# Attention stage of a fused two-layer kernel: values three groups behind the scores, maxima by halves of the keys, row sums in one row, weight splitting on GpSimd, the factor of q where q is rounded

## The chip, the cores and the metric

The kernel runs as one program on one core of a Trainium2 chip. The metric is device microseconds from launch to end of that core, and less is better. The core has TensorE (PE in the rows, PEld for its weight loads), VectorE (DVE), ScalarE (ACT), GpSimd (POOL) and the queue of SyncE (SP), which issues every DMA of this kernel. The engines run their own instruction lists in order and meet only at semaphores.

## The reference, cut to what matters

Two layers of a transformer over 2048 tokens of width 128: an RWKV mixer and two mixtures of experts, then attention between two gated networks with integer weights. The change touches the attention alone. What it computes (residual additions and layer norms stand around it):

```
qkv = rms_norm(x, gamma) @ w_qkv             # x: 2048 x 128, 16 heads of 64
q, k, v = split(qkv);  q = q * 64 ** -0.5
sim = einsum("bhid,bhjd->bhij", q, k)        # 2048 x 2048 for each head
attn = softmax(sim, axis=-1)
out = einsum("bhij,bhjd->bhid", attn, v)
return out @ w_out
```

Everything is float32. The kernel feeds TensorE with pairs of a rounded high part and a remainder (tiles that end in `_h` and `_l`, or `hi` and `lo`), and so gets near float32 from passes of the faster rounded type.

## The kernel before, in words

**Units of work.** A head is worked in four chunks c = 0..3 of 512 queries (CH, NC). A chunk has eight groups g = 0..7, each of 256 keys. I call "step (c, g)" what TensorE does from the scores of one group to the scores of the next. A loop runs over pairs of heads: an even head (par = 0) and an odd one (par = 1); heads 0, 1, 14 and 15 are written out around it. The file's own function `main_chunk` stands once for each engine, and the order of the code is the order of the engine's list.

**One step on TensorE.** `scores_t`: four passes of 512 columns that give transposed scores of 256 keys by 512 queries, with the negative row maxima as a 65th row of `qb`. Then `score_pair` of the *next* head: two passes that give the untransposed scores of 128 queries by 1024 keys in banks 4 and 5, only so that VectorE can take their maximum. Then `values`: four passes with the probabilities of the group PV_LAG behind. That is ten passes for a plain step. At places set by SPARE something is added: `project_v` and `project_qk` for the next heads, `turn_maxima` (a small transpose), `column_sums`, and `project_out` (one float32 product, two passes).

**The other engines in a step.** ScalarE takes the exponential twice, to `p_raw` and rounded to `p_h`. GpSimd subtracts them to `p_l` (`low_part`). VectorE adds up a quarter of a chunk's row sums (`whole_sum` in groups 0 to 3 for the chunk before, `first_half_sum` in groups 4 to 7) and takes the maximum of each score pair (`maximum`). A pair may be written only when the maximum before it is done (`s_max`), `values` waits for `p_h` and `p_l`, and `low_part` for `p_h`.

**Maxima.** Each head needs 32 pairs: 16 tiles of 128 queries by two halves of the keys, before in the order tile 0 half 0, tile 0 half 1, tile 1 half 0 and so on. PAIRS_OF_MAXIMA says how many pairs stand in each step. The rows of the change show its first chunk; in the other three there is one in every step.

**Sums.** `column_sums` turns the row sums `l_sum` (128 partitions x 512) into a [128, 4] column by four float32 products with a column of ones. `invert` takes the reciprocal on VectorE from PSUM. SP stores it (`store_inverse`), loads it back spread over 128 partitions (`load_inverse`), and GpSimd multiplies the attention output by it (`scale`). `project_out` and `add_out` follow.

**Projections.** Heads two ahead are projected in chunk 3. ScalarE copies the high part (`high_qk`), VectorE the low part (`low_qk`), and SP moves them by six DMAs for each 512 tokens to the places that the products want (`move_high`, `move_low`); the fourth part is done at the start of the next window. `high_qk_weights`/`low_qk_weights` split the weights of a head, `low_v_weights` those of a pair; q's factor of 1/8 was applied there.

**What sets the order.** Only these lists and the tables:

```
PV_LAG = 2
PAIRS_OF_MAXIMA = ((0, 0, 1, 1, 1, 2, 1, 2), (1,) * 8, (1,) * 8, (1,) * 8)
V_SPLIT = ((0, 3), (1, 0))
SCALE_GROUP = 1
COPY_GROUP = 1
```

## Time and profile before

| what | value |
|---|---|
| median of 3 runs | 2335.62 us (2335.23 to 2339.02) |
| the profiled execution, own time | 2329.67 us |
| its span, first to last instruction | 2327.9 us |
| first scores of head 0 | 674.8 us into the span |
| heads 2 to 13 | 872.6 to 2088.0 us: 1215.4 us, 12 heads |
| mean granted TensorE clock | 0.936 |

The profiled execution lies 5.95 us under the median of the timed runs, and 1.8 us of its own time lie outside the span. About 1600 us of the span are attention, in sixteen windows of about 100 us that repeat nearly to the hundredth. So a microsecond per head is worth some 15 us. In a timeline row the number in brackets is the idle time of the engine just before the instruction and what ended it. The length of a matmul row is modelled, and passes overlap: the distance of two starts tells what one costs.

### The profile page before, as it was taken

How to read it: one execution, taken by the hardware profiler on the slowest of the kernel's cores; microseconds unless marked ns; L12 is line 12 of the kernel's file. 1: busy time of each engine (PE TensorE's matmuls, PEld its weight loads, DVE VectorE, ACT ScalarE, POOL GpSimd, SP SyncE). 2: the span in 40 equal slices, each digit the busy share in tenths (PEclk: the TensorE clock that was granted, in tenths of full speed). 3: DMA queues.
4: the chain of work that ended last, by engine and by line, in shares of the span. 5: the costliest groups of instructions: out<-in, count | busy, mean ns of one | idle time of the engine just before them, and what ended most of it. 6: DMA issues, size and time to landing. Idle time of an engine off the chain costs nothing.

```text
span 2327.9 us, 30823 instructions
## 1 busy us (share of the span) xinstructions
PE 2109.7 (91%) x8706; PEld 1563.0 (67%) x8706; DVE 1862.4 (80%) x2037; ACT 1487.5 (64%) x1834; POOL 1407.1 (60%) x635
## 2 busy tenths in 40 slices
PE   6999469998779999999999999999999999999987
PEld 4777247776747676766767676676767667676654
DVE  5888867886378887888888788888888888888875
ACT  4666426664337676766777676766767667676773
POOL 1000100003038887888788788888888888888992
PEclk7999659997679999999999999999999999999997
DMA  3210003100310221303022120302212021220000
GB/s 116 62 45 18 0 0 74 45 27 15 80 31 12 64 47 38 64 14 69 12 64 48 37 64 13 69 17 60 59 26 64 18 65 26 50 64 17 10 1 18
DMA packets 68662, 94.55 MB, mean 41 GB/s; under 512 B 23200, under 2 KB 26656, under 8 KB 68256
## 3 DMA queue, kind: packets, MB, share of 16 engines
q1 hardware_dynamic: 68528, 92.80, 17.0%
q8 instruction: 80, 1.31, 0.2%
q14 instruction: 54, 0.44, 0.1%
HBM read 40.99 MB, written 1.30 MB: 18 GB/s over the span
## 4 chain that ended last, share of the span: by engine, by line
PE 66%; DVE 15%; issue 7%; ACT 4%; SPq 3%; POOL 3%; DMA 2%; DVEq 0%; ACTq 0%; POOLq 0%
PE ps L656 8%; PE ps L678 8%; PE ps L679 7%; PE ps L693 7%; PE ps L696 7%; PE ps L545 6%; PE ps L547 5%; PE ps L546 5%; DVE m_part L1365 4%; PE ps L706 4%; DVE l_sum L1359 3%; SPq L336 2%; POOL p_l L467 2%; PE ps L527 2%; ACT p_h L1041 2%
## 5 line engine op out<-in xcount | busy, mean ns | idle before, releaser
L467 POOL TENSOR_TENSOR p_l<-p_raw,p_h 128x1024 fp32r<-128x1024 f32 x512 | 1242.7, 2445 | 287.9 <-ACT p_h L1041 241.4
L1038 ACT ACTIVATE p_raw<-ps 128x1024 f32<-128x1024 f32 x512 | 564.2, 1102 | 409.1 <-PE ps L679 404.7
L1365 DVE TENSOR_REDUCE m_part<-ps 128x1 f32<-128x1024 f32 x480 | 585.7, 1220 | 215.5 <-PE ps L656 214.6
L1041 ACT ACTIVATE p_h<-ps 128x1024 fp32r<-128x1024 f32 x512 | 522.3, 1020 | 0.0
L678 PE MATMUL ps<-qa,ka 128*128 128x512 f32 x1024 | 448.6, 438 | 11.0 <-ACT p_h L1041 4.8
L693 PE MATMUL ps<-p_h,v_hl 128*128 128x512 f32 x1024 | 416.9, 407 | 29.0 <-POOL p_l L467 27.9
L679 PE MATMUL ps<-qb,kb 65*128 65x512 f32 x1024 | 412.9, 403 | 0.0
L1359 DVE TENSOR_REDUCE l_sum<-p_raw 128x128 f32<-128x1280 f32 x256 | 376.7, 1475 | 0.4
L656 PE MATMUL ps<-ka,qa 128*128 128x512 f32 x960 | 317.4, 412 | 52.2 <-DVE m_part L1365 32.9
L696 PE MATMUL ps<-p_l,v_hl 128*64 128x512 f32 x1024 | 325.5, 399 | 0.0
L1345 DVE TENSOR_REDUCE p_raw<-p_raw 128x128 f32<-128x1024 f32 x256 | 308.9, 1208 | 12.4 <-ACT p_raw L1038 12.4
L693 PEld LDWEIGHTS ps<-p_h,v_hl 128*128 128x128 f32 x1024 | 196.0, 191 | 143.4 <-issue 62.4
L656 PEld LDWEIGHTS ps<-ka,qa 128*128 128x128 f32 x960 | 177.1, 193 | 127.3 <-DVE m_part L1365 68.6
L929 ACT ACTIVATE big<-ps,b 128x512 f32<-128x512 f32 x256 | 175.3, 688 | 117.6 <-PE ps L547 117.6
L678 PEld LDWEIGHTS ps<-qa,ka 128*128 128x128 f32 x1024 | 199.0, 194 | 74.2 <-issue 33.8
L679 PEld LDWEIGHTS ps<-qb,kb 65*128 65x128 f32 x1024 | 197.9, 193 | 53.5 <-issue 15.8
L696 PEld LDWEIGHTS ps<-p_l,v_hl 128*64 128x64 f32 x1024 | 140.6, 137 | 67.6 <-issue 3.0
L1188 DVE TENSOR_TENSOR h_l<-big,h_h 128x512 fp32r<-128x512 f32 x256 | 165.6, 688 | 5.1
L443 POOL MEMSET ones<- 128x128 f32 x1 | 0.2, 204 | 247.3 <-DVE x L1202 247.3
L441 POOL TENSOR_TENSOR cen<-big 128x2048 f32<-128x2048 f32 x1 | 4.5, 4530 | 230.2 <-ACT big L947 230.2
L706 PEld LDWEIGHTS ps<-ones,l_sum 128*128 128x128 f32 x472 | 114.6, 325 | 5.4 <-issue 3.5
L1208 DVE CAST h_h<-big 128x512 fp32r<-128x512 f32 x128 | 54.6, 427 | 68.3 <-ACT big L929 68.3
(185 smaller groups left out, 2790.8 us busy)
## 6 DMA issues: line engine op xcount, KB each, us to landing
big<-g_scratch SPq DMA_DIRECT2D x64, 256.0 KB, 3.2
xnp<-r_scratch SPq DMA_DIRECT2D x59, 256.0 KB, 3.8
qa<-qk_hi SPq DMA_DIRECT2D x112, 128.0 KB, 2.4
ka<-qk_hi SPq DMA_DIRECT2D x56, 128.0 KB, 2.4
kb<-qk_hi SPq DMA_DIRECT2D x56, 128.0 KB, 2.4
ka<-xnp SPq DMA_DIRECT2D x28, 128.0 KB, 2.4
qb<-xnp SPq DMA_DIRECT2D x28, 128.0 KB, 2.4
ka<-qk_low SPq DMA_DIRECT2D x28, 128.0 KB, 2.4
```

Source lines behind the costliest of these rows:

```text
L467: nc.gpsimd.tensor_tensor(p_l[:, g % 4, :, :], slots(g), p_h[:, g % 4, :, :].bitcast(fp32), ALU.subtract).then_inc(pl_done, 1)
L656: last = mm(ps[:, 4 + b, :], qa[par][:, it * 128:it * 128 + 128], ka[par][:, chunk(2 * half + b)], start=True, stop=True)
L678: mm(st, ka[par][:, jt * 128:jt * 128 + 128], qa[par][:, ds(c * CH, CH)], start=True, stop=False)
L679: last = mm(st, kb[par][:, jt * 128:jt * 128 + 128], qb[par][:, ds(c * CH, CH)], start=False, stop=True)
L693: return mm(ps[:, bank, :], v_hl[:, par, 2 * g + j, :], p_h[:, g % 4, j, :], start=start, stop=stop)
L696: return mm(ps[0:DH, bank, :], v_hl[:, par, 2 * g + j, 0:DH], p_l[:, g % 4, j, :], start=False, stop=False)
L706: last = mm(ps[:, bank, t:t + 1], l_sum[:, :].rearrange("p (q t) -> p t q", t=TPC)[:, t, :], ones[:, 0:1], start=True, stop=True)
L1038: af(slots(g), s_t, ACT.Exp).then_inc(raw_done, 1)
L1041: af(p_h[:, g % 4, :, :], s_t, ACT.Exp).then_inc(ph_done, 1)
L1345: nc.vector.tensor_reduce(p_raw[:, ACC, cols, 0], p_raw[:, 0:ACC, cols, :].rearrange("p g n b -> p n g b"), AX.XY, ALU.add).then_inc(half_ ...
L1359: nc.vector.tensor_reduce(l_sum[:, cols], p_raw[:, ACC:GROUPS + 1, cols, :].rearrange("p g n b -> p n g b"), AX.XY, ALU.add).then_inc(all_ ...
L1365: nc.vector.tensor_reduce(m_part[:, it, half:half + 1], ps[:, 4:6, :].rearrange("p b n -> p (b n)"), AX.X, ALU.max).then_inc(s_max, 1)
```

## The change

- **PV_LAG 2 to 3.** `values` of group g - 3 follows the scores of group g. SCALE_GROUP goes from 1 to 3 and COPY_GROUP from 1 to 2.
- **Maxima by halves.** The first eight query tiles take all first halves of the keys, then all second ones (PAIR_AT). Head h+1's first pair is now in step (0, 1) and wants key chunks 0 and 1 alone; chunks 2 and 3 are wanted at pair 8, in step (1, 0). Step (0, 5) has one pair in place of two.
- **Projections later.** Part 0 of q and k goes to step (3, 3), part 1 to (3, 5), part 2 to (3, 7), part 3 to (0, 1); their low parts to (3, 4), (3, 6), (0, 0) and (0, 2).
- **Row sums.** One float32 product with a column of 1/128 gives a row [1, 512]; ScalarE copies it (`row_sums`), SP stores it and loads it back as [128, 4]; VectorE inverts that from SBUF in step (c, 0) of the chunk after. The factor 128 is taken out in `add_out`.
- **Weights.** `low_qk_weights` and `low_v_weights` go from VectorE to GpSimd, at its step (1, 1). One `qk_raw` in place of two. The factor of q is applied where q is rounded, from a column `qk_scale`, in `high_qk` and `low_qk`.

```diff
-PV_LAG = 2
+PV_LAG = 3
-PAIRS_OF_MAXIMA = ((0, 0, 1, 1, 1, 2, 1, 2), (1,) * 8, (1,) * 8, (1,) * 8)
+PAIRS_OF_MAXIMA = ((0, 1, 1, 1, 1, 1, 1, 2), (1,) * 8, (1,) * 8, (1,) * 8)
+PAIR_AT = ([(it, 0) for it in range(8)] + [(it, 1) for it in range(8)]
+           + [(it, half) for it in range(8, NT) for half in range(2)])
-LATE_LOW = 1
-INVERT_GROUP = (6, 6, 6, 4)
+LATE_LOW = {0: 2, 2: 3}
+LATE_QK = 1
...
 @block.sync
+            def store_sums(head, c):
+                sp.wait_ge(l_done, chunk_of(head, c) + 1)
+                sp.dma_start(l_scratch[ds(head, 1), chunk(c)], l_row[:, :]).then_inc(l_stored, 16)
+            def load_sums(head, c):
+                sp.wait_ge(l_stored, 16 * (chunk_of(head, c) + 1))
+                sp.dma_start(l_col[:, c % 2, :], l_scratch[ds(head, 1), chunk(c)].rearrange("a (p t) -> (a p) t", p=128)).then_inc(l_loaded, 16)
...
 @block.gpsimd
+            def low_qk_weights(par, head):
+                pool.wait_ge(qkw_hi, head + 1)
+                nc.gpsimd.tensor_tensor(qk_l[par][:, :, :], qk_raw[:, :, :], qk_h[par][:, :, :].bitcast(fp32),
+                                        ALU.subtract).then_inc(qkw_lo, 1)
...
 @block.tensor
-                for t in range(TPC):
-                    last = mm(ps[:, bank, t:t + 1], l_sum[:, :].rearrange("p (q t) -> p t q", t=TPC)[:, t, :], ones[:, 0:1],
-                              start=True, stop=True)
-                last.then_inc(l_ps, 1)
+                mm(ps[0:1, bank, :], inv_c[:, 0:1], l_sum[:, :], start=True, stop=True).then_inc(l_ps, 1)
...
 @block.scalar
+            def row_sums(head, c, bank):
+                k = chunk_of(head, c)
+                act.wait_ge(l_ps, k + 1)
...
+                af(l_row[:, :], ps[0:1, bank, :], ACT.Copy).then_inc(l_done, 1)
...
 @block.vector
-                tt(lo.bitcast(fp32r), ps[:, bank, :], hi, ALU.subtract).then_inc(lo_done, 1)
+                stt(lo.bitcast(fp32r), ps[:, bank, :], qk_scale[:, 0:1], hi, ALU.mult, ALU.subtract).then_inc(lo_done, 1)
-                dve.wait_ge(l_ps, k + 1)
+                dve.wait_ge(l_loaded, 16 * (k + 1))
-                nc.vector.reciprocal(r_col[:, c % 2, :], ps[:, bank, 0:TPC]).then_inc(r_ready, 1)
+                nc.vector.reciprocal(r_col[:, c % 2, :], l_col[:, c % 2, :]).then_inc(r_ready, 1)
-                tt(x[:, chunk(c)], x[:, chunk(c)], ps[:, bank, :], ALU.add).then_inc(out_add, 1)
+                stt(x[:, chunk(c)], ps[:, bank, :], 1.0 / C, x[:, chunk(c)], ALU.mult, ALU.add).then_inc(out_add, 1)
```

**TensorE, step (0, 5) of an even head in the loop.** Before, from the first score pair to the sums (L656 is the pair, L693 and L696 the values, L706 the sums):

```order
L656 MATMUL ps<-ka,qa 128x512 [waits s_max]
L656 MATMUL ps<-ka,qa 128x512
L693 MATMUL ps<-p_h,v_hl 128x512 [waits pl_done,ph_done]
L696 MATMUL ps<-p_l,v_hl 64x512 x2
L693 MATMUL ps<-p_h,v_hl 128x512
L654 REGISTER_ALU
L656 MATMUL ps<-ka,qa 128x512 [waits s_max]
L656 MATMUL ps<-ka,qa 128x512
L704 ISA [waits mt_done]
L706 MATMUL ps<-ones,l_sum 128x1 [waits all_sum]
L706 MATMUL ps<-ones,l_sum 128x1 x3
```

The same step of the changed kernel (L695 is the pair, L732 and L735 the values, L744 the sums):

```order
L695 MATMUL ps<-ka,qa 128x512 [waits s_max]
L695 MATMUL ps<-ka,qa 128x512
L732 MATMUL ps<-p_h,v_hl 128x512 [waits pl_done,ph_done]
L735 MATMUL ps<-p_l,v_hl 64x512 x2
L732 MATMUL ps<-p_h,v_hl 128x512
L743 ISA [waits mt_done]
L744 MATMUL ps<-l_sum,inv_c 1x512 [waits all_sum]
```

The second pair with its own wait for `s_max` is gone from the step, and four products of one column have become one of 512 columns.

**VectorE, from the last maximum of chunk 0 into chunk 1 of an even head.** Before (L1318 to L1324 split the weights, L1359 is the row sum, L1383 the residual addition):

```order
L1365 TENSOR_REDUCE m_part<-ps 128x1 [waits s_ps]
L1317 ISA
L1318 SCALAR_TENSOR_TENSOR qk_l<-qk_raw,qk_h 128x64 [waits qkw_hi]
L1320 TENSOR_TENSOR qk_l<-qk_raw,qk_h 128x64
L1323 REGISTER_ALU
L1324 TENSOR_TENSOR wv_hl<-wv_raw,wv_hl 128x128 [waits vw_hi]
L1353 ISA
L1354 REGISTER_ALU [waits raw_done]
L1359 TENSOR_REDUCE l_sum<-p_raw 128x128 [waits l_ps,half_sum]
L1383 TENSOR_TENSOR x<-x,ps 128x512 [waits out_ps]
```

The changed kernel at that place (L1401 is the maximum, L1395 the row sum, L1419 the addition, L1415 the reciprocal):

```order
L1401 TENSOR_REDUCE m_part<-ps 128x1 [waits s_ps]
L1389 ISA
L1390 REGISTER_ALU [waits raw_done]
L1395 TENSOR_REDUCE l_sum<-p_raw 128x128 [waits l_ps,half_sum]
L1419 SCALAR_TENSOR_TENSOR x<-ps,x 128x512 [waits out_ps]
L1412 REGISTER_ALU
L1415 RECIPROCAL r_col<-l_col 128x4 [waits o_scaled,l_loaded]
L1400 REGISTER_ALU
L1401 TENSOR_REDUCE m_part<-ps 128x1 [waits s_ps]
```

The weight splits have left VectorE's list here, and the reciprocal has come in ahead of the first maximum, with a wait for a DMA (`l_loaded`).

**SP, chunks 0 and 1 of an even head.** Before, from the row of maxima to the load of the inverse:

```order
L318 ISA
L320 DMA qb<-m_t 1x12x128 [waits mt_done]
L323 ISA
L324 ISA [waits r_ready]
L324 DMA r_scratch<-r_col 128x4
L327 REGISTER_ALU
L328 DMA xnp<-r_scratch 128x512 [waits r_stored]
```

The changed kernel from the same DMA on:

```order
L328 DMA qb<-m_t 1x12x128 [waits mt_done]
L331 REGISTER_ALU
L332 ISA [waits l_done]
L332 DMA l_scratch<-l_row 1x512
L335 REGISTER_ALU
L336 DMA l_col<-l_scratch 128x4 [waits l_stored]
L340 DMA r_scratch<-r_col 128x4 [waits r_ready]
L344 DMA xnp<-r_scratch 128x512 [waits r_stored]
```

Each chunk's sums now take two more DMAs, one behind the other, ahead of the two of the inverse.

## Rows read from the trace of the kernel before

**Rows 1.** The page: span, and busy time of each engine.

```profile
span 2327.9 us, 30823 instructions
PE 2109.7 (91%) x8706; PEld 1563.0 (67%) x8706; DVE 1862.4 (80%) x2037; ACT 1487.5 (64%) x1834; POOL 1407.1 (60%) x635
```

**Rows 2.** Windows: length, busy PE, PEld, DVE, ACT, POOL; clock, DMA share, GB/s.

```profile
872.60:2088.00 1215.40, 1148.86 (x4801) 846.85 (x4800) 1022.19 (x967) 849.42 (x955) 1017.54 (x445) 0.98 0.20 44
2182.40:2268.30 85.90, 75.04 (x281) 46.47 (x279) 66.83 (x49) 66.17 (x70) 83.31 (x35) 1.00 0.00 1
1281.22:1382.94 101.72, 97.90 (x425) 73.35 (x425) 83.25 (x79) 71.30 (x82) 83.43 (x37) 0.98 0.20 41
1382.94:1482.16 99.22, 92.04 (x378) 66.40 (x376) 86.32 (x82) 70.29 (x78) 85.69 (x39) 1.00 0.22 48
```

**Rows 3.** The chain of work in head 6: start, length, what.

```profile
1326.72 1.64 PE ps L706 x8
...
1334.45 0.86 PE ps L715 x2
...
1336.24 0.47 PE ps L656 x2
```

**Rows 4.** Timeline of PE, head 7: steps (0, 3) and (0, 5).

```profile
1390.84 0.39 PE L679 MATMUL ps<-qb,kb 65*128 65x512 f32 x1
1392.42 0.73 PE L656 MATMUL ps<-ka,qa 128*128 128x512 f32 x2 [1.20 <-DMA qb<-qk_low]
...
1398.83 0.39 PE L693 MATMUL ps<-p_h,v_hl 128*128 128x512 f32 x1
1399.62 0.73 PE L656 MATMUL ps<-ka,qa 128*128 128x512 f32 x2 [0.40 <-DVE m_part L1365]
```

**Rows 5.** Timeline of DVE and PE, head 7: into step (1, 1).

```profile
1409.05 1.02 DVE L1318 SCALAR_TENSOR_TENSOR qk_l<-qk_raw,qk_h 128x64 fp32r<-128x64 f32 x1
...
1411.60 0.40 PE L679 MATMUL ps<-qb,kb 65*128 65x512 f32 x1
1413.46 0.73 PE L656 MATMUL ps<-ka,qa 128*128 128x512 f32 x2 [1.46 <-DVE m_part L1365]
```

**Rows 6.** Timeline of PE, head 7: steps (1, 4) and (2, 4).

```profile
1421.36 0.63 PE L656 MATMUL ps<-ka,qa 128*128 128x512 f32 x2
1423.07 0.47 PE L693 MATMUL ps<-p_h,v_hl 128*128 128x512 f32 x1 [1.08 <-POOL p_l L467]
...
1446.31 0.47 PE L693 MATMUL ps<-p_h,v_hl 128*128 128x512 f32 x1 [0.98 <-POOL p_l L467]
```

**Rows 7.** Windows, head 6, columns as in rows 2: a stretch of low clock.

```profile
1301.60:1304.80 3.20, 3.20 (x9) 2.26 (x8) 2.35 (x2) 1.86 (x2) 2.53 (x2) 0.50 0.23 11
```

**Rows 8.** Groups by line, heads 2 to 13: count, busy us, mean ns, idle before.

```profile
L467 POOL TENSOR_TENSOR p_l<-p_raw,p_h 128x1024 fp32r<-128x1024 f32 x385 | 933.7, 2441 | 198.9 <-ACT p_h L1041 160.6 <-issue 37.2
L1365 DVE TENSOR_REDUCE m_part<-ps 128x1 f32<-128x1024 f32 x385 | 469.8, 1220 | 167.7 <-PE ps L656 166.9
...
L1359 DVE TENSOR_REDUCE l_sum<-p_raw 128x128 f32<-128x1280 f32 x192 | 283.1, 1475 | 0.0
...
L1027 ACT ACTIVATE xnp<-ps 128x512 f32<-128x512 f32 x48 | 29.3, 610 | 14.1 <-PE ps L693 14.1
...
L1335 DVE TENSOR_TENSOR qk_low<-ps,qk_hi 128x512 fp32r<-128x512 f32 x24 | 16.5, 689 | 16.7 <-ACT qk_hi L997 16.7
...
L1318 DVE SCALAR_TENSOR_TENSOR qk_l<-qk_raw,qk_h 128x64 fp32r<-128x64 f32 x12 | 12.0, 998 | 0.0
```

**Rows 9.** Before the attention, GpSimd idle: timeline, and one line's ns min/median/max.

```profile
613.55 0.22 DVE L1318 SCALAR_TENSOR_TENSOR qk_l<-qk_raw,qk_h 128x64 fp32r<-128x64 f32 x1
...
L1314 DVE SCALAR_TENSOR_TENSOR xnp<-xnp,gamma,ps x4: 749/750/750, 601.9 to 610.5; 128x512 f32<-128x512 f32 x4
```

**Rows 10.** DMA issues: count, size, median us from issue to landing.

```profile
r_scratch<-r_col SPq DMA_DIRECT2D x59, 2.0 KB, 1.7
...
mix<-in_mix SPq DMA_DIRECT2D x1, 2.5 KB, 2.9
```

More of the change, by code:

```diff
@@ L135, in macaron_kernel @@
         p_l = sb("p_l", [128, 4, 2, CH], fp32r, two)
-        qk_raw = [sb(f"qk_raw{i}", [C, 2, DH], where=two) for i in range(2)]
+        qk_raw = sb("qk_raw", [C, 2, DH], where=two)
+        qk_scale = sb("qk_scale", [128, 1], where=two)
         qk_h = [sb(f"qk_h{i}", [C, 2, DH], fp32r, two) for i in range(2)]
@@ L362, in window @@
                 for c in range(NC):
-                    summed = before(head, c, 1)
+                    scaled, summed = before(head, c, 2), before(head, c, 1)
+                    if c == 0 and late_project:
+                        move_high(head + 1, 1 - par, 2, qk_hi)
+                        move_low(head + 1, 1 - par, 2, qk_low[0])
+                    if exists(scaled[0]) and not (last and c > 0):
+                        store_inverse(*scaled)
+                        load_inverse(*scaled)
                     if c == 0 and late_project:
@@ L494, in window @@
                             low_v(head + 1, 1 - par)
+                        if (c, g) == (1, 1) and project:
+                            low_qk_weights(par, head + 2)
+                            if par == 0:
+                                low_v_weights(pair + 1)
             def attention():
+                low_qk_weights(0, 0)
+                low_v_weights(0)
+                low_qk_weights(1, 1)
                 low_v(0, 0)
@@ L862, in attention @@
                 window(PAIRS - 1, 1, False, False, False)
-                for g in (GROUPS - 2, GROUPS - 1):
+                for g in range(GROUPS - PV_LAG, GROUPS):
                     values(HEADS - 1, 1, NC - 1, g)
@@ L1058, in main_chunk @@
                             turn_maxima(head + 1 - n, n, spare_bank(c))
+                        elif kind == "sums":
+                            row_sums(*summed, spare_bank(c))
                         elif kind == "v":
@@ L1078, in attention @@
                 high_parts(3)
-                for head in range(2):
-                    high_qk_weights(head, 1)
+                high_qk_weights(0, 0)
                 high_v_weights(0)
+                high_qk_weights(1, 1)
                 for head in range(2):
@@ L1418, in main_chunk @@
                     if g == 0:
[L1419 removed]
+                        scaled, added = before(head, c, 2), before(head, c, 3)
                         if c > 0 and exists(added[0]) and not last:
@@ L1452, in attention @@
                 low_parts(3)
-                for head in range(2):
-                    low_qk_weights(head, head)
-                low_v_weights(0)
                 for head in range(2):
```

132 lines of the change are left out of this document (65 added, 67 removed).

## Prediction

> **What bounds the kernel now.** I read the page first: TensorE is busy 91% of the span, VectorE 80%, GpSimd 60% [rows 1]. That averages stages in which GpSimd has no work, so the windows come next. In heads 2 to 13 TensorE is busy 1149 of 1215 us, VectorE 1022, GpSimd 1018, ScalarE 849 [rows 2]. Per head that is 101.3 us with 95.7, 85.2, 84.8 and 70.8 busy. Nobody is saturated, and the two behind TensorE stand 16 us lower. So I ask how much of a head is TensorE's own work and how much is waiting that the busy column hides.
>
> The unit of price is the distance of two starts. In the chain a score pair of two 512-column passes advances 0.47 us, 0.235 a pass; the sums' eight pieces take 1.64, and the two passes of a float32 product of 512 columns 0.86 [rows 3]. A plain step of ten passes is 2.35, thirty-two of them 75 us. Five things above that touch the change.
>
> - Step (0, 3): a pair is due at 1390.84 + 0.235 and starts at 1392.42, 1.35 late, behind the DMA that brings the last keys [rows 4].
> - Step (0, 5): the second pair, due at 1399.06, starts at 1399.62, 0.56 late, behind the first one's maximum [rows 4].
> - The sums: 1.64 a chunk [rows 3].
> - Step (1, 1): the pair is due at 1411.83 and starts at 1413.46, 1.63 late. VectorE had the weight split, 1.02 us, ahead of its row sum [rows 5].
> - Steps (1, 4) and (2, 4) of an odd head: values are due 0.47 after the pair, at 1421.83, and start at 1423.07, 1.24 late, behind GpSimd. The second place has 0.98 of idle where the first has 1.08, so 1.14 [rows 6]. I looked for both in even heads and found none.
>
> The low clock is a sixth. One window of head 6 has the clock at 0.50, 1.2 GHz, right after the long sums of step (0, 5) and their waits [rows 7]; before it the engine had gaps in which it waited. Over the twelve heads the mean is 0.98 [rows 2]: 2% of 1215 us, 24 us of full-speed work lost, with 0.005 of rounding 18 to 30.
>
> **The change part by part**, for a pair of heads, now 202.6 us (1215.4 / 6).
>
> Keys by halves: the wait in (0, 3) goes, 2 x 1.35 = 2.7. The second half is wanted in step (1, 0), seven steps after the projection of part 3, over 16 us; six issues and a landing fit many times. A first pair a step earlier wants part 1, projected in (3, 5) and split in (3, 6), two steps ahead.
>
> One pair in (0, 5): 2 x 0.56 = 1.1. The other double, in (0, 7), stays.
>
> Row sums in one product: 1.64 - 0.86 = 0.78 for each of eight chunks, 6.2. No row shows one stationary column with 512 moving ones; bounds are 0.47 (two plain passes) and 1.64 (no gain). It is nearest to the float32 product of 512 columns. ScalarE gets a copy of 512 elements, 0.61 as its others [rows 8], and is idle 30 of 101 us [rows 2].
>
> Weight split off VectorE: 2 x 1.63 = 3.3. On GpSimd it is 128 columns: an eighth of the 2.44 us for 1024 is 0.31 [rows 8], and with a fixed part at most twice that. Three per pair are 0.9 to 1.8 us, in an engine with 16 us to spare per head. Here row and rule are worth weighing. The split took 0.22 us with GpSimd idle [rows 9] and 0.998 on average in the loop [rows 8]. The Trainium skill, page "SBUF — State Buffer", section "Who interferes with whom", says that a DVE instruction with two SBUF inputs and a GpSimd instruction that reads SBUF lock each other out for a whole instruction; the trace agrees. By that rule a new instruction that reads `hi` and `qk_scale` from SBUF could be locked out too, if the column counts as an input; the page does not say. It is rival 3.
>
> Values one group later: the two waits of an odd head go, 1.24 + 1.14 = 2.4 once per pair. GpSimd is late there because it splits v in step (1, 0) and scales in step 1; a third step of lag is 2.35 us of room, more than either wait. ScalarE needs the buffer of group n - 4 for group n, which values release a step before it is asked: no new wait.
>
> VectorE's additions: the low parts go from 0.689 (one SBUF input, GpSimd busy, [rows 8]) to the 0.75 of the same form with a column [rows 9], and I take the same for `add_out`, whose form changes alike: 16 x 0.06 = 1.0 a pair, against 2 x 1.2 removed. The reciprocal, 0.2, moves into step (c, 0). All of it is under TensorE, which after the change works 94 us in the even head (101.7 less 1.35, 0.56, 3.1, 1.63 and a low-clock stretch of about 1) and 90 in the odd one (99.2 less 6.6 and 2.4), where VectorE has 83 and 86 [rows 2].
>
> The new wait: `invert` stands in step (c, 0) ahead of that step's maximum, and behind the maximum TensorE's next pair is queued. From the end of the sums in step 5 it takes the copy 0.6 [rows 8], the store 1.7, the load 2.9 (rows of 16 bytes per partition; the row of 20 bytes, [rows 10]) and some 0.3 of hand-over, 5.5. Meanwhile TensorE does steps 6 and 7 with one `project_out`, 5.6, and VectorE a row sum and the addition, 1.475 + 0.7 [rows 8]: 7.7. Margin 2.2; in chunks 1 and 3, with the sums a step earlier, more. SP's extra store and load stand between part 0's moves and part 1's, and are through before part 1 is split. Cost nothing.
>
> One place loses: at the start of the attention the weights of head 1 are loaded only after head 0's are split, in one buffer: a load of the 2.9 us kind [rows 10] in front of ScalarE's first copy. Part of it lies beside head 0's projection; I take 1.2.
>
> The sum: 2.7 + 1.1 + 6.2 + 3.3 + 2.4 = 15.7 a pair, 94 for heads 2 to 13. Heads 0, 1 and 14 have most of it, about 1.3 pairs: 20. Head 15 is GpSimd's, 83.3 of 85.9 busy [rows 2], and gains nothing. The clock: shorter sums and fewer gaps; I take half of 24, 12, plus 3 for the other heads. Minus 1.2. Together 128. The profiled execution's 2329.7 becomes 2202, and its median of runs, 6 us higher, 2208.
>
> Both bounds: with the sums at no gain (-44) and no clock (-15) 69 are left, 2267; with the cheapest sums (+22) and all the clock (+15) it is 165, 2171.
>
> **The rivals.**
>
> 1. *The gain runs into the engines behind.* After the change an odd head has 90 us of TensorE's work, 86.3 of VectorE's less 1, and 85.7 of GpSimd's plus 0.5 [rows 2]. In groups 0 to 3 VectorE has a row sum of 1.475 and a maximum of 1.22 [rows 8] against a step of 2.35: where TensorE no longer waits for GpSimd, it will for the maximum. For it: today in step (1, 1) this wait shows. Against: the sums of groups 4 to 7 are a fifth shorter, there `project_out` and the sums lengthen TensorE's steps, and VectorE catches up. Price: the 2.4 and a third of the other 13.3, 7 per pair, 50 in all: about 2258.
> 2. *More than the sum.* All half-clock stretches go, and small waits between the places with them: 2171 or a little under.
> 3. *The column locks VectorE out.* Each low split waits for one GpSimd instruction, 0.78 as L1318 did, up to 2.44: four a head, 15 heads, 47 to 146 us. Mean case 2255, worst 2354, and then slower. Against: L1335, with one SBUF tensor, runs at 0.689 beside a busy GpSimd [rows 8]; only the column is new.
> 4. *Slower, by the chain of the row sums.* If the load of 128 pieces of 16 bytes lands late by more than 2.2, VectorE stands in every step (c, 0), and TensorE behind it. With x us beyond the margin in two chunks and x - 2.35 in the other two, 15 heads lose 60x - 70. It eats the 128 us at x = 3.3: a load of 8.4 us where 2.9 is the nearest row. From there it is slower; at 10 us the loss is 224, the time 2430.
> 5. *No change:* some other wait takes the whole place. Nothing in the rows is that long.
>
> **How the numbers follow.** Forecast (2175 to 2240) 0.66; rival 1 (2240 to 2300) 0.17; rival 2 0.06; rival 3 short of slower 0.03; slower by 3, 4 or something unseen 0.07; no change 0.01. The range takes the forecast's own and half of each neighbour: 2165 to 2264, which is also what the two bounds span. A timing of this kernel tells about 0.2% from nothing, 5 us: faster 0.92, same 0.01, slower 0.07.
>
> **What the changed profile would show.** Right: twelve heads in some 1110 us, PEclk 0.99 or 1.00 over them; the sums' line with two rows a chunk and 0.86 in the chain; no pair behind a DMA in chunk 0; `values` behind GpSimd seldom; `qk_l` on GpSimd at 0.3 to 0.45; the low split at 0.75; the load of `l_col` landing in about 3 us and no idle before the reciprocal. Wrong: idle before the reciprocal beyond 0.3, the low split over 1 us, or TensorE's pair behind `m_part` in steps 2 to 4 of each chunk, which is rival 1.

## The result and the profile after

The changed kernel takes 2213.17 us (median of 3 runs, 2211.21 to 2218.78) where the kernel before takes 2335.62. The ratio is 0.9477, with a 95% interval of 0.9447 to 0.9507. The forecast was 2208, its range 2165 to 2264. The profiled execution's span went from 2327.9 [rows 1] to 2208.7 us, so 119.2 us less. Its page:

```profile
span 2208.7 us, 30463 instructions
PE 2034.0 (92%) x8352; PEld 1451.9 (66%) x8352; DVE 1846.7 (84%) x1997; ACT 1523.8 (69%) x1877; POOL 1414.5 (64%) x660
PEclk7999758998778999999999999999999999999998
```

The windows of heads 2 to 13 and of the stretch from head 15 to the end, to be read against the first row of [rows 2] (columns as there):

```profile
855.20:1969.20 1114.00, 1090.46 (x4514) 756.59 (x4513) 999.00 (x937) 879.61 (x991) 1022.83 (x462) 1.00 0.23 48
2056.00:2208.70 152.70, 120.06 (x437) 78.96 (x435) 113.52 (x99) 87.30 (x109) 96.92 (x47) 0.88 0.03 9
```

Twelve heads fell from 1215.4 to 1114.0 us. TensorE is now busy in 1090 of them and the mean clock is 1.00 (0.98 before). Heads 0, 1 and 14 fell from 292.2 to 267.3. But from the start of head 15 to the end it is 152.7 us where it was 145.5.

What TensorE waits for in heads 2 to 13 (us in total, times, longest):

```profile
PE ps L717 <- issue: 13.7, 5, 3.0
PE ps L695 <- DVE m_part L1401: 9.8, 25, 0.4
```

Before, the same view had 28.0 us behind VectorE's maxima, 14.9 behind the DMA and 14.3 behind GpSimd. The last two are gone, and no group for VectorE's maxima has a wait over 0.4. New is the first line: 5 waits of up to 3.0 us in which TensorE has nothing that the profile names.

The groups by line of the same stretch, against [rows 8]:

```profile
L490 POOL TENSOR_TENSOR p_l<-p_raw,p_h 128x1024 fp32r<-128x1024 f32 x384 | 931.1, 2460 | 91.2 <-ACT p_h L1085 81.6 <-issue 9.5
L1401 DVE TENSOR_REDUCE m_part<-ps 128x1 f32<-128x1024 f32 x384 | 467.4, 1217 | 113.1 <-PE ps L695 112.6
...
L744 PE MATMUL ps<-l_sum,inv_c 128*1 128x512 f32 x96 | 48.9, 590 | 0.0
...
L1371 DVE SCALAR_TENSOR_TENSOR xnp<-ps,qk_scale,qk_hi 128x512 fp32r<-128x512 f32 x24 | 17.9, 745 | 0.0
L1415 DVE RECIPROCAL r_col<-l_col 128x4 f32<-128x4 f32 x48 | 8.1, 168 | 0.0
L501 POOL TENSOR_TENSOR qk_l<-qk_raw,qk_h 128x128 fp32r<-128x128 f32 x12 | 5.7, 474 | 0.0
```

The reader is to see four things. The sums are two rows a chunk (96 in 48 chunks). The low part with the column of factors takes 0.745 us, as forecast. The reciprocal has no idle time before it, so the trip of the sums through DRAM is in time. And GpSimd, though its 2.46 us a step are the same as before, stood idle ahead of them for 91 us and not 199: it works nearly without gaps. That last line turned out to matter most.

### The profile page after: what moved, and what is told of

It reads as the page before. It is cut to its first block and busy times, and to the rows that moved or that the text cites. A ratio compares the mean times of both kernels' runs of the same rounds, so it can differ in the third digit from the quotient of the medians.

```text
span 2208.7 us, 30463 instructions
## 1 busy us (share of the span) xinstructions
PE 2034.0 (92%) x8352; PEld 1451.9 (66%) x8352; DVE 1846.7 (84%) x1997; ACT 1523.8 (69%) x1877; POOL 1414.5 (64%) x660
## 5 line engine op out<-in xcount | busy, mean ns | idle before, releaser
L1401 DVE TENSOR_REDUCE m_part<-ps 128x1 f32<-128x1024 f32 x480 | 584.3, 1217 | 143.9 <-PE ps L695 143.3
L717 PE MATMUL ps<-qa,ka 128*128 128x512 f32 x1024 | 447.4, 437 | 15.7 <-issue 13.7
L732 PE MATMUL ps<-p_h,v_hl 128*128 128x512 f32 x1024 | 404.2, 395 | 1.5 <-POOL p_l L490 1.3
L1395 DVE TENSOR_REDUCE l_sum<-p_raw 128x128 f32<-128x1280 f32 x256 | 377.0, 1476 | 0.4
L695 PE MATMUL ps<-ka,qa 128*128 128x512 f32 x960 | 315.1, 409 | 12.3 <-DVE m_part L1401 12.3
L735 PE MATMUL ps<-p_l,v_hl 128*64 128x512 f32 x1024 | 321.5, 395 | 0.0
L732 PEld LDWEIGHTS ps<-p_h,v_hl 128*128 128x128 f32 x1024 | 194.1, 190 | 77.9 <-issue 4.9
L695 PEld LDWEIGHTS ps<-ka,qa 128*128 128x128 f32 x960 | 172.7, 190 | 90.0 <-DVE m_part L1401 56.7
L735 PEld LDWEIGHTS ps<-p_l,v_hl 128*64 128x64 f32 x1024 | 138.6, 135 | 71.8 <-issue 1.5
L584 PE MATMUL ps<-h_h,w_l 128*128 128x512 f32 x256 | 103.9, 406 | 0.8
```

Of the source, the lines that this page charges most:

```text
L695: last = mm(ps[:, 4 + b, :], qa[par][:, it * 128:it * 128 + 128], ka[par][:, chunk(2 * half + b)], start=True, stop=True)
L717: mm(st, ka[par][:, jt * 128:jt * 128 + 128], qa[par][:, ds(c * CH, CH)], start=True, stop=False)
L732: return mm(ps[:, bank, :], v_hl[:, par, 2 * g + j, :], p_h[:, g % 4, j, :], start=start, stop=stop)
L735: return mm(ps[0:DH, bank, :], v_hl[:, par, 2 * g + j, 0:DH], p_l[:, g % 4, j, :], start=False, stop=False)
L1395: nc.vector.tensor_reduce(l_sum[:, cols], p_raw[:, ACC:GROUPS + 1, cols, :].rearrange("p g n b -> p n g b"), AX.XY, ALU.add).then_inc(all_ ...
L1401: nc.vector.tensor_reduce(m_part[:, it, half:half + 1], ps[:, 4:6, :].rearrange("p b n -> p (b n)"), AX.X, ALU.max).then_inc(s_max, 1)
```

## The experiments

Each is timed against the kernel before on the same chip. The ratios are compared with the change's 0.9477; 0.001 of ratio is 2.3 us. "Loop" is the time from the first scores of head 2 to those of head 14 in the profiled execution: 1215.4 before, 1114.0 after. A loop figure is that of one execution, and stretches of low clock differ between executions, so a few us of it are noise. "Half clock" is a granted clock of 0.50, 1.2 GHz.

| run | median us | ratio, 95% | loop | head 15 to end |
|---|---|---|---|---|
| undo_sums | 2261.32 | 0.9697 (0.9649 to 0.9745) | 1156.8 | 153.2 |
| undo_split | 2295.35 | 0.9819 (0.9770 to 0.9867) | 1182.3 | 161.0 |
| undo_lag | 2290.47 | 0.9816 (0.9770 to 0.9861) | 1179.4 | 149.0 |
| lag_as_before | 2267.97 | 0.9726 (0.9692 to 0.9760) | 1161.3 | 144.3 |
| stand_in | 2249.84 | 0.9640 (0.9616 to 0.9663) | 1143.6 | 160.4 |
| before_halves | 2330.31 | 0.9986 (0.9963 to 1.0009) | 1208.7 | 143.1 |
| before_split | 2319.36 | 0.9942 (0.9920 to 0.9964) | 1212.4 | 143.1 |
| unroll_pe | 2203.42 | 0.9448 (0.9428 to 0.9468) | 1101.3 | 157.6 |
| end_gpsimd | 2209.13 | 0.9467 (0.9450 to 0.9484) | 1120.1 | 146.4 |
| move_double | 2226.53 | 0.9546 (0.9527 to 0.9566) | 1122.2 | 151.6 |
| double_later | 2206.05 | 0.9459 (0.9431 to 0.9488) | 1104.4 | 155.0 |
| best | 2169.56 | 0.9298 (0.9272 to 0.9324) | 1084.3 | 145.7 |

The theory to test was the prediction's: each part takes its own wait or product off TensorE's path, and the parts add up. The rival was that they hang together, so that a part alone, or the change less one part, is worth something else.

### undo_sums: the old row sums in the changed kernel

```diff
...
-                mm(ps[0:1, bank, :], inv_c[:, 0:1], l_sum[:, :], start=True, stop=True).then_inc(l_ps, 1)
+                for t in range(TPC):
+                    last = mm(ps[:, bank, t:t + 1], l_sum[:, :].rearrange("p (q t) -> p t q", t=TPC)[:, t, :], inv_c[:, 0:1],
+                              start=True, stop=True)
+                last.then_inc(l_ps, 1)
...
```

The rest of the edit takes the copy on ScalarE and the two DMAs out and puts the reciprocal in steps 6, 5, 6, 5.

> The changed kernel with the row sums as before: four products of one column each on TensorE, the reciprocal read from PSUM by VectorE in steps 6, 5, 6, 5, no row on its way through DRAM and no copy of it on ScalarE; all else stays changed. If the sums are paid on TensorE's path in each chunk: the step with the one-row product lasts 3.42 us against 2.32 of a plain one in the changed trace, the old step 4.05, so 0.6 to 0.8 us more in each of 60 chunks, 36 to 48 us more, 2249 to 2261 us, and the step (c, 5) back at 4.0. The rival, that the sums' step hides behind other engines' work because ScalarE and VectorE carry less here (no row copied, 0.59 us a chunk off ScalarE): under 15 us more, 2213 to 2228.

The time is 2261 us, at the upper end of what the first theory gives, and the step with the sums is back from 3.4 to 3.98 to 4.2 us. The chunk's sums are on TensorE's path. The steps alone make 0.6 to 0.7 us a chunk, 5 a pair of heads; the loop grew by 42.8 us, 7.1 a pair. Most of the rest is the clock: eight stretches of half clock, 3.4 us each, begin in the loop, where the changed kernel has three. Another 3.5 us are a new wait, of the transpose of the maxima (`turn_maxima`) for VectorE.

### undo_split: the splitting of the weights on VectorE again

```diff
                 main_chunk(pair, par, 0, has_next, project, late_project)
+                if project:
+                    low_qk_weights(par, 2 * pair + par + 2)
+                    if par == 0:
+                        low_v_weights(pair + 1)
```

Here `low_qk_weights` is two TENSOR_TENSOR of 128x64, in every head, and `low_v_weights` one of 128x128, in even heads alone. They stand where they stood before; the first was then a SCALAR_TENSOR_TENSOR with the factor of q. GpSimd's are gone.

> The changed kernel with the splitting of the weights of q, k and v on VectorE again, at the end of chunk 0, behind the two maxima of step (0, 7), in its old place. If VectorE's lateness there reaches TensorE as the prediction has it (1.63 us a head): the wait of the scores' pair in step (1, 1), 0.65 us in the changed trace, grows to 1.5 to 2.3, which makes 0.8 to 1.63 us a head and 12 to 24 us in 14 heads: 2225 to 2237 us. The rival, that with the values three steps behind VectorE has slack there: the same time within 5 us, 2208 to 2218.

Both expectations missed. It is 82 us over the changed kernel, the most of all for the least work. The loss is in the even heads: their step (1, 1) takes 10.0 to 12.7 us where it took 2.97, that of the odd heads 4.1 to 4.7. The timelines of VectorE, of GpSimd and of TensorE at the start of chunk 1 of head 4 (start, length, what, idle time before and its releaser; "x4" are four in a row):

```profile
1088.35 1.10 DVE L1371 TENSOR_TENSOR qk_l<-qk_raw,qk_h 128x64 fp32r<-128x64 f32 x1
1089.38 2.47 DVE L1372 TENSOR_TENSOR qk_l<-qk_raw,qk_h 128x64 fp32r<-128x64 f32 x1
1091.77 2.50 DVE L1376 TENSOR_TENSOR wv_hl<-wv_raw,wv_hl 128x128 fp32r<-128x128 f32 x1
1094.20 1.47 DVE L1400 TENSOR_REDUCE l_sum<-p_raw 128x128 f32<-128x1280 f32 x1
...
1086.96 9.57 POOL L490 TENSOR_TENSOR p_l<-p_raw,p_h 128x1024 fp32r<-128x1024 f32 x4
...
1097.52 1.22 PE L691 MATMUL ps<-ka,qa 128*128 128x512 f32 x2 [6.23 <-DVE m_part L1406]
```

Four of GpSimd's low parts stand without a gap, 2.4 us each, so they end near 1089.4, 1091.7 and 1094.1. VectorE's three end at 1089.45, 1091.85 and 1094.27: each gets through only as one of GpSimd's ends. Work of 0.2 to 0.3 us costs 2.5, the three together 5.9, and TensorE's pair waits 6.2 us for the maximum behind them. The row sum that follows, with one SBUF input, has its usual 1.47 us in the middle of GpSimd's next one. The Trainium skill, page "SBUF — State Buffer", section "Who interferes with whom", says just this: a DVE instruction with two SBUF inputs contends with a GpSimd instruction that reads SBUF, and one of them blocks for the whole instruction. The trace agrees. In the kernel before, GpSimd had a gap there: the first of VectorE's took 1.02 us in head 7 [rows 5], and the one behind it 0.21 on average.

Of the 68.3 us that the loop grew, 49.0 are waits behind VectorE's maxima (58.8 where 9.8 stood). The other 19.2 are longer busy time of TensorE: the waits are followed by half clock, 81.9 us of it in the loop where the changed kernel has 10.2. Outside the loop the run lost another 11.5 us in heads 0 and 1, and 8.3 in head 15, of which end_gpsimd tells.

### stand_in: VectorE equally late, without the second input

```diff
...
+                    for i in range(3):
+                        nc.vector.tensor_reduce(spare_col[:, i:i + 1], inv_c[:, :].rearrange("p (a n) -> p a n", a=1).to_broadcast([128, 4, 128]),
+                                                AX.XY, ALU.max)
...
```

> The changed kernel with the splitting of the weights still on GpSimd, and, in the old place of it on VectorE (end of chunk 0), three maxima over 512 constant columns each, whose result nothing reads: about 1.8 us of VectorE's time a head with one SBUF input instead of two. It asks what made the run with the split back on VectorE 82 us slower. If it was VectorE's busy time there (the prediction's term, 1.63 us a head): 14 times at most 1.8 us, up to 25 us more, 2213 to 2238 us, with (1, 1) longer by the same amount in every head. If it was that the splitting waits for GpSimd's running operation because both read SBUF through two inputs (2.5 us in the row of one of 128x64 that takes 0.2 alone), the even head of each pair shows nothing of its 7 to 9 us in (1, 1), and the time stays under 2240. A rival, that any delay of VectorE at this place starts a longer one (a late maximum, then TensorE's clock): 2270 to 2300 here too.

VectorE's line for the stand-in, and TensorE's waits behind its maxima, in the loop:

```profile
L1483 DVE TENSOR_REDUCE spare_col<-inv_c 128x1 f32<-128x512 f32 x36 | 22.4, 676 | 0.0
...
PE ps L696 <- DVE m_part L1402: 32.3, 27, 2.2
```

Three reductions of 0.68 us never wait for GpSimd, and nothing like the 9 us is there: step (1, 1) of an even head has 4.7 to 5.1 us in place of 10 to 12.7. (In the odd heads it has 4.7 to 6.0, where undo_split with its two splits has 4.1 to 4.7.) So the length of undo_split's waits is the meeting with GpSimd. But the time, 2249.84 us, lies outside every range given: 37 us over the changed kernel, more than the 25 allowed for, and less than the rival's. The loop alone grew by 29.6, 2.5 a head for 1.9 us of work: 22.5 of it are waits behind the maxima, the rest mostly the half clock that follows them (nine stretches begin in the loop, not three). At this place VectorE has no slack. In the profiled execution another 7.7 us are in head 15, far from the edit.

### undo_lag and lag_as_before: the values two groups behind

```diff
-PV_LAG = 3
+PV_LAG = 2
...
-LATE_LOW = {0: 2, 2: 3}
+LATE_LOW = {0: 2, 1: 3}
```

> The changed kernel with the values two groups behind the scores (PV_LAG 2 in the place of 3) and, so that the bank is free in step (0, 2), the low part of block 3 of q and k one step earlier on VectorE. If the distance is what took the waits for GpSimd away: the products of the low part wait again for GpSimd behind its extra work in steps (1, 4) and (2, 4) of the odd head and, new, in step (1, 2) behind the split of the weights; 2.4 us a pair of heads at least, 5 with the new place, so 17 to 40 us more, 2230 to 2253 us, and a group of waits for POOL on the products with the low part. The rival, that only the wait changed its name and the odd head's steps get their time from elsewhere: the same within 5 us, and no such group.

At 2290 us it is outside both, because it measured more than it should. The waits for GpSimd came back (16.7 us in the loop), but the larger part is another: step (0, 2) grew from 2.3 to between 4.4 and 6.0 us in every head, 23.1 us of waits for VectorE's maximum, because the moved low part stands ahead of it and waits for ScalarE's copy. That is the experiment's own wait, so I repeated it with everything that belongs to the distance as it was before:

```diff
...
-         ((3, "qk", 0), (4, "sums", 0), (5, "qk", 1), (6, "out", 0), (7, "qk", 2)))
+         ((2, "qk", 0), (3, "sums", 0), (4, "qk", 1), (5, "out", 0), (6, "qk", 2)))
-LOW_QK = {(3, 4): 0, (3, 6): 1}
+LOW_QK = {(3, 3): 0, (3, 5): 1, (3, 7): 2}
...
```

> The changed kernel with the values two groups behind the scores and with all that goes with it as before: the list of chunk 3 (q and k in steps 2, 4, 6), the low parts in (3, 3), (3, 5), (3, 7) and (0, 1), the fourth block projected in step 0, the copy and the scaling in step 1, the last addition in (3, 6). It repeats the run with PV_LAG 2, whose 77 us were mostly a wait of 2 to 3 us in step (0, 2) that its own placing of the low part made. The prediction's term for the distance alone is 2.4 us a pair, 17 us: 2225 to 2240. A rival: the distance also covers the VectorE work of chunk 0 and GpSimd's extra work, so that waits for GpSimd come back in five or more places, 20 to 60 us more than the changed kernel by the halves-only run's rise of such waits from 9.5 to 18.1 us in eight heads: 2240 to 2275.

TensorE's waits in its loop:

```profile
PE ps L732 <- POOL p_l L490: 37.7, 36, 1.5
PE ps L695 <- DVE m_part L1401: 10.1, 27, 0.7
PE ps L717 <- ACT p_h L1085: 6.2, 4, 1.7
PE ps L717 <- issue: 1.8, 1, 1.8
```

The rival's range holds it. With two groups of distance 36 products of the values wait for GpSimd's low part in the loop, 37.7 us. With three there is not one. The loop is 47.3 us longer, 7.9 a pair, where the prediction priced the distance at 2.4. The two places that it priced, steps (1, 4) and (2, 4) of the odd head, have 14.8 us of these waits, 2.5 a pair, so their price was right. The other 22.9 us stand in four places that had 1.2 us in the kernel before: step (0, 4) of both heads, (0, 6) of the even and (1, 3) of the odd one. GpSimd has more to do in the changed kernel and TensorE reaches it sooner; the two waits of [rows 6] are those that showed while other waits still held TensorE back.

### before_halves and before_split: two parts alone on the kernel before

```diff
...
-                it, half = q // 2, q % 2
+                it, half = PAIR_AT[q]
...
```

> The kernel before with one edit: the pairs of scores for the maxima ordered by halves of the keys (eight tiles of queries against the first half, then against the second, then alternating), the first turn's maximum in step (1, 4) in the place of (1, 0) since it needs 12 pairs. The numbers of pairs in each step stay those of before. If the prediction's term stands (the wait for the moves by DMA in chunk 0, 14.9 us in heads 2 to 13, and 2.7 us a pair): about 2.7 us a pair, 16 in the loop, 19 in all with the others, 2313 to 2322 us, and no pair that waits for a DMA. The rival, that the wait comes from the copy on ScalarE and VectorE's low part and so stays under another name: 2330 to 2340 us.

The waits of TensorE in heads 2 to 13 of this run:

```profile
PE ps L696 <- POOL p_l L470: 28.0, 34, 1.1
PE ps L659 <- DVE m_part L1368: 27.3, 36, 1.6
PE ps L681 <- ACT p_h L1044: 7.7, 5, 1.8
```

The 14.9 us behind the DMA are gone, as the prediction has it, and the time hardly moves: the interval of the ratio includes 1. Waits for GpSimd rose from 14.3 to 28.0 us: of the 14.9, 13.7 stand under another name, 13.0 of them in step (0, 4), where the kernel before has none. (The five for ScalarE are the turns of TensorE's loop; before, 4.3 us stood there and 4.2 under "issue".) The loop gains 6.7 us, some of it from the clock: nine stretches of half clock where there were thirteen. The rival had the time right and the engine wrong.

> The kernel before with one part of the change: the splitting of the weights on GpSimd in step (1, 1), and so the factor of q at the copy and at VectorE's low part. If the prediction's term holds alone (1.63 us a head off the wait in step (1, 1), which is 1.6 to 2.1 us there): 14 times 1.6, 23 us less, 2308 to 2316 us. The rival, that the parts need each other (GpSimd, now 0.7 us later in chunk 1 with the values only two steps behind, gives it back on the products of the low part): 0 to 12 us less, 2323 to 2336. What speaks for it is the order by halves, which took its DMA waits away and gave all but 5 us back to waits for GpSimd.

Its edit puts `low_qk_weights` and `low_v_weights` behind GpSimd's step (1, 1), and the factor of q where q is rounded. TensorE's waits in the loop:

```profile
PE ps L712 <- POOL p_l L470: 23.5, 21, 1.5
PE ps L675 <- DMA qb<-qk_low: 16.7, 12, 1.6
PE ps L675 <- DVE m_part L1384: 14.2, 36, 0.4
PE ps L697 <- issue: 10.7, 5, 2.4
```

The waits behind VectorE halved, from 28.0 to 14.2, and step (1, 1) fell from 4.0 to 5.4 us to 2.97. Yet the loop is only 3.0 us shorter, where the term was 20 (3.3 a pair). The median, 2319.36 us, lies between the two ranges; by the ratio the whole kernel gained 13.5 us. GpSimd takes back 9.2 of the 13.8 us, the DMA 1.8 and the turns of the loop 2.2 (10.7 where 8.5 stood), of which the next run tells. The profiled execution is 12.5 us shorter as a whole; 9.5 of them lie outside the loop, spread over four stretches, and I can't assign them.

### unroll_pe: TensorE's loop written out

```diff
-                with pe.Fori(1, PAIRS - 1) as pair:
+                for pair in range(1, PAIRS - 1):
```

In the changed kernel, at the turn from head 3 to head 4, TensorE's timeline has:

```profile
1038.01 0.40 PE L586 MATMUL ps<-x_l,qk_h 128*128 128x512 f32 x1
1040.92 0.47 PE L717 MATMUL ps<-qa,ka 128*128 128x512 f32 x1 [2.51 <-issue]
```

Behind three of the five turns the clock then falls to 0.50 (1.2 GHz) for 3.4 us, after the engine had been idle.

> The changed kernel with TensorE's program for pairs of heads 1 to 6 written out in place of its loop; the other engines keep their loops. If the 2.65 to 3.0 us for which TensorE has nothing in flight at the loop's turn are the loop's own (fetching or jumping), five of them go, and the 1.6 us of half clock behind three of them: 15 to 20 us less, 2193 to 2198 us, step (3, 7) at 3.4 in each odd head. The rival, that another engine's loop holds TensorE at that point or that the written-out program has to be fetched at the same cost: no more than 4 us less, 2209 to 2216, and the idle time is still at step (3, 7), or spread over other steps.

The line with "issue" is gone from the waits, step (3, 7) is 3.42 us everywhere, and no stretch of half clock begins in the loop: 1101.3 us, 12.7 less. So the idle time is the loop's own. It is not the whole 15 to 20, since in five of the six even heads step (0, 3) now has 1.1 us more behind VectorE, whose low part waits for ScalarE's copy. ScalarE is late there from the start of the head on. TensorE's last product of the first scores of head 4, and ScalarE's first exponential of them:

```profile
1038.97 0.39 PE L718 MATMUL ps<-qb,kb 65*128 65x512 f32 x1
...
1041.22 1.10 ACT L1082 ACTIVATE p_raw<-ps 128x1024 f32<-128x1024 f32 x1 [2.07 <-PE ps L718]
```

The scores are done at 1039.36, and ScalarE starts 1.86 us later, with nothing from another engine outstanding that the profile shows. So it is in the even heads 4 to 12, each behind a turn of ScalarE's own loop; in head 2, behind none, the delay is 0.2 us. The time of 2203 us lies between the expectations, also because the last head fell out 4.9 us longer.

### end_gpsimd: the last head's scaling on GpSimd

In the changed kernel's last head the timelines of TensorE, VectorE and GpSimd have:

```profile
2080.43 2.05 PE L853 MATMUL ps<-xnp,w_o 128*128 128x512 f32 x2 [5.29 <-DVE xnp L1433]
...
2075.29 5.00 DVE L1433 TENSOR_TENSOR xnp<-xnp 128x512 f32<-128x512 f32 x1
...
2070.18 9.56 POOL L490 TENSOR_TENSOR p_l<-p_raw,p_h 128x1024 fp32r<-128x1024 f32 x4
```

It is the pattern of undo_split: a product of two SBUF inputs, 0.69 us alone, ends 0.55 us after GpSimd's row of four. All five of these multiplications of one kernel, minimum, median and maximum in ns, first in lag_as_before and then in the changed kernel:

```profile
L1433 DVE TENSOR_TENSOR xnp<-xnp x5: 693/1690/1703, 2137.1 to 2210.5; 128x512 f32<-128x512 f32 x5
...
L1433 DVE TENSOR_TENSOR xnp<-xnp x5: 693/2964/8274, 2075.3 to 2158.7; 128x512 f32<-128x512 f32 x5
```

GpSimd's gaps decide it. In lag_as_before it stands idle for about 0.5 us shortly ahead of each of the first four, and they take 1.1 to 1.7 us. In the changed kernel it has no gap there, and they take 5.0, 2.7, 8.3 and 3.0. The distance of the values is not the whole of it: undo_lag has two groups too, with GpSimd's scaling in step 3, and its first multiplication takes 5.0 us without a gap, the next three, each behind one of 0.5, take 1.7. In the runs with three groups and this code unedited the last head varies from 151.6 to 161.0 us, with multiplications of 0.7 to 8.3 us; the surpluses of undo_split and stand_in there are of this kind.

```diff
...
+                        if last and g == 5:
+                            end_scale(c)
...
```

VectorE's call of `end_scale` for these chunks is gone.

> The changed kernel with the last head's scaling of the output (o_raw by r_bc, two SBUF inputs) on GpSimd behind its step 5 in chunks 0 to 3; the last one stays on VectorE. In the changed trace steps (0, 7) and (2, 7) of head 15 last 8.4 and 10.1 us, (1, 7) 4.4, of which TensorE waits 5.3 for the 5.0 us that VectorE's multiplication takes. If that wait is VectorE's for GpSimd's SBUF reads, the multiplication on GpSimd takes 1.31 us as its like in the loop does and the wait goes: 7 to 12 us less, 2201 to 2206 us. The rival, that GpSimd is the bound in the last head (its low part takes 2.44 a step against 1.86 of TensorE's step) and every microsecond given to it comes back: between 3 us less and 5 more, 2210 to 2218.

The last head went from 152.7 to 146.4 us, TensorE's waits ahead of the products of the scaled output from 19.4 to 12.8, by whatever name. The median, 2209.13 us, lies between both expectations, 4 us under the changed kernel, and the interval does not part it from the change. In the profiled execution nothing was gained as a whole, since its loop is 6.1 us longer, some 3.4 of it because five turns were followed by half clock, three in the other. What is left of the wait is GpSimd's own queue: the scaling stands behind the low part of step 5.

### move_double and double_later: the second maximum of step (0, 7)

```diff
-PAIRS_OF_MAXIMA = ((0, 1, 1, 1, 1, 1, 1, 2), (1,) * 8, (1,) * 8, (1,) * 8)
+PAIRS_OF_MAXIMA = ((0, 1, 1, 1, 1, 1, 1, 1), (1,) * 8, (1, 1, 1, 1, 1, 1, 2, 1), (1,) * 8)
```

> The changed kernel with the second maximum of step (0, 7) moved to step (2, 6). The wait of 0.65 us in step (1, 1), for the maximum behind it, is there in every head. If VectorE's two maxima in a row in (0, 7) cause it, (1, 1) falls from 2.97 to 2.3 and the double costs in (2, 6) what it costs in (0, 7) on TensorE (1.19): 0.65 a head, 5 to 10 us less, 2203 to 2208 us. The rival, that the wait comes from the addition and the reciprocal that stand ahead of the maximum in (1, 0) and (1, 1): the same within 3 us, 2210 to 2216, or more where (2, 6) of the even head already has 3.72 us and GpSimd behind it.

Slower, outside both ranges. Steps (0, 7) and (1, 1) gave 1.12 and 0.65 us a head, as expected, but TensorE then reached the projection of v in step (1, 3) of the even head before GpSimd had split its weights in its own step (1, 1):

```profile
PE ps L681 <- POOL wv_hl L506: 6.5, 6, 1.1
```

and in the odd head the second pair in (2, 6) made VectorE late for the step behind it, (2, 7), by 0.64 us. The next version has the double in (2, 5), its scores behind the sums, and GpSimd's split in step (1, 0):

> The changed kernel with the second maximum of step (0, 7) in step (2, 5), its scores behind the row of sums, and GpSimd's splitting of the weights one step earlier, in (1, 0). The run with it in (2, 6) took 1.1 us from (0, 7) and 0.65 from (1, 1) in every head, and lost it to a wait of 1.1 us for that splitting in (1, 3) of the even head, to 1.1 us in (2, 6) and to 1 us behind it where VectorE came late. If these are the causes, (1, 3) stays at 3.8, and (2, 5) costs 0.5 us more, since VectorE has slack there: 1.3 us a head, 15 to 20 us less, 2193 to 2200 us. The rival, that GpSimd (92% busy in the loop) is the bound as soon as TensorE gains 1.5 us: waits for its low part come up, and the time stays within 4 us of 2213, or above.

The loop is 9.6 us shorter, heads 0, 1 and 14 2.7, and waits for GpSimd's low part are 0.3 us in all. The run's stretch ahead of the attention was 5.6 us longer than the change's, in code that no edit touches, so the medians show 7 of the 12. 2206.05 us lies between the two ranges. What the second pair saves in chunk 0 it costs in part again: 1.1 us a head in steps (2, 5) and (2, 6), where 0.5 was expected.

### best: the three together

> The changed kernel with three edits together: the loop over pairs of heads written out on all five engines, the last head's scaling on GpSimd, and the second maximum in step (2, 5) with the splitting in (1, 0). Alone they measured 9.8 us (TensorE's loop only), 4.0 and 7.1 us less than the changed kernel. If TensorE's path holds all three, as their step tables have it (12.7 us in the loop for the first, 6.3 in the last head, 12.3 in heads 0 to 14), they add: 21 to 31 us less, 2182 to 2192 us, and the 1.4 us in step (0, 3) of the even head, which TensorE's written-out loop got and which the other engines' loops would explain, goes too. The rival, that GpSimd at 86.5 us of work a head takes over as the bound: waits for its low part on the products, and 2193 to 2203 us.

2169.56 us, 0.9298 of the kernel before and 44 us under the changed one, with all five loops written out. That is 12 us below the range expected. The same two windows as of the changed kernel, and all that TensorE waits for in heads 2 to 13:

```profile
847.00:1931.30 1084.30, 1079.65 (x4513) 754.30 (x4512) 997.87 (x937) 877.75 (x991) 1023.27 (x462) 1.00 0.23 49
2017.30:2163.00 145.70, 120.42 (x437) 81.94 (x436) 95.38 (x95) 86.94 (x109) 100.99 (x51) 0.87 0.03 10
...
PE ps L703 <- DVE m_part L1409: 4.7, 12, 0.4
```

TensorE is busy 1079.7 of 1084.3 us. The 1.1 us in step (0, 3) are gone, and ScalarE's first exponential now starts within 0.1 us of its scores in all six even heads, so the five waits came from ScalarE's turns. No stretch of half clock begins in the loop. By their own stretches the single edits were worth 31.3 us (12.7 in the loop, 6.3 in the last head, 12.3 in heads 0 to 14); here the attention is 39.3 us shorter, 7.4 of the surplus in the loop, where the five waits in step (0, 3) stood. Another 6.4 us lie ahead of the attention, where executions of unedited code differ by such amounts. No run writes ScalarE's loop out alone.

## Why the prediction was right, and where not

In total 128 us were forecast for the profiled execution and 119.2 measured. No large misses cancel in that: heads 2 to 13 gave 101.4 of 106, heads 0, 1 and 14 gave 24.9 of 23, and head 15 lost 7.2. By its own steps:

- **Heads 2 to 13**: 94 plus 12 of clock, measured 101.4. Thirteen stretches of half clock began there before, three after, at some 1.6 us each: 16 us. The other 85 are the steps. The waits for other engines and the DMA, without the loop's turn, fell from 57.2 us to 9.8, by 47; the four terms for them add up to 57.
- **Row sums**: mis-sized. Taken at 0.86 us, they advance TensorE by 1.03, as the rows below have it: 1.26 us from the last product of the values to the next scores, less the 0.235 of that product. Step (2, 5) went from 4.05 to 3.37, a saving of 0.68 and not 0.78. The upward surprise of undo_sums, 7.1 a pair, is the clock with it, and a wait for VectorE.
- **Keys by halves, one pair in (0, 5)**: both waits are gone. But the first one alone gives 13.7 of its 14.9 us back to waits for GpSimd; those don't exist in the changed kernel.
- **Weight split, 3.3 a pair**: a term without a size of its own. It is 0.5 a pair in the loop on the kernel before and 11.4 (68.3 / 6) in the changed one, 8.2 in waits and 3.2 in half clock. The prediction took the wait behind the 0.998 of L1318 as a fixed price, although it told of the lockout that makes it depend on GpSimd; it did not ask how often GpSimd would be in the middle of an instruction after the change.
- **Values later, 2.4 a pair**: right for the two places it names, 2.5 in lag_as_before. The distance and what belongs to it are worth 7.9 in the changed kernel, since 3.8 a pair of waits in four further places would be there without it.
- **The step that failed** is that the terms may be added. In the loop the three undone parts cost 42.8, 68.3 and 47.3 us, 158 for a change worth 101 (in medians 48, 82 and 55, 185 for 122). TensorE waits for whichever engine is latest, so a part's worth depends on the others. The sum came out near since it was read from waits that the whole change takes away together: that is my reading of the numbers, and no run tests it. Keys by halves and the single pair in (0, 5) were not taken out of the changed kernel alone.
- **Loop's turn**: not in the prediction. "issue" and ScalarE together had 8.5 us before, the turn now has 13.7; 5 us lost.
- **Head 15 "gains nothing"**: it lost 7.2. TensorE's waits for GpSimd's low part fell there from 10.6 us to 0.5, but 17.7 of waits for the multiplication took the place of 4.2. The same lock between VectorE and GpSimd, which rival 3 looked for at the low part with its column, sat at a line that the change does not touch.
- **Start of the attention**: a loss of 1.2 us was forecast, none came: 674.8 before, 674.7 after.
- **Rivals**: 3 is out (0.745 us beside a busy GpSimd); 4 is out (the load of `l_col` lands in 1.6 us, not 2.9); 1 didn't come: its sign, pairs behind VectorE's maximum in steps 2 to 4, shows once in the loop, with 0.4 us, and best shows that even 30 us less in the loop doesn't bring it; 2 didn't come either, three stretches of half clock were left.

The rows to the second point, TensorE's timeline of the changed kernel, head 5, step (1, 4):

```profile
1150.73 0.39 PE L732 MATMUL ps<-p_h,v_hl 128*128 128x512 f32 x1
1151.04 1.02 PE L744 MATMUL ps<-l_sum,inv_c 128*1 128x512 f32 x2
1151.99 0.50 PE L717 MATMUL ps<-qa,ka 128*128 128x512 f32 x1
```

Open is why the turn of TensorE's loop costs what it does. The idle time at a turn is 1.4 to 2.3 us in the kernel before, 1.5 to 1.8 in lag_as_before and 2.5 to 3.0 in the changed kernel. The distance of the values doesn't decide it: undo_lag, with two groups, has 2.5 to 2.9. Like the changed kernel, and unlike the other two, it has a projection of q and k in the last step before the turn. That is a coincidence in the record and no more; no run moves the projection alone.

## What to carry to other kernels

When several engines take turns as the latest, price a change as a whole from the waits that go together, and expect a part tried alone to show little; a part that looks worthless alone can be what makes another one pay. Ask of each engine that will be relieved or filled which gaps close by it, and list the two-input VectorE instructions that used those gaps, also those far from the edit. And look at a loop's turn on the engine that bounds the kernel: it is a few microseconds that no line owns, here often with a slower clock behind them.

## What the runs showed of the hardware that was not expected

- A VectorE TENSOR_TENSOR with two SBUF inputs beside a GpSimd without gaps can miss more than one turn: 8.3 us for work of 0.69, longer than three of GpSimd's instructions.
- A column of factors as scalar operand doesn't make an instruction such a one: 0.745 us from PSUM, column and one SBUF tensor, beside GpSimd at 92%.
- The turn of a loop left TensorE idle for 1.4 us at the least and 3.3 at the most. Half clock followed for 3.4 us behind two (double_later) to all (end_gpsimd, move_double) of the five turns. ScalarE's turn showed as a start 1.8 to 2.0 us late.
- A float32 product with one stationary column has rows as long as a square one (590 and 592 ns), and it costs more: 1.15 us of TensorE's steps, (2, 5) and the one behind it, where the square product of `project_out` costs 0.89 in (2, 7) and the one behind it.
